# Up biases as the last row of the experts' weights, loads of 126 partitions, another order of products, and integer targets in the rows of a decoder layer's expert stage

## The chip, the cores and the metric

The kernel runs on one core of a Trainium2 chip. The metric is the device time of one execution in microseconds (us); less is better. The engines are named as in the profile: PE (TensorE) does matrix products, PEld is its loading of stationary operands, DVE is VectorE, ACT is ScalarE, POOL is GpSimd and SP is SyncE, which here only starts DMAs.

## The reference

One decoder layer with post-norms on x of shape (16, 128, 128): self-attention with 16 heads of 8, whose four projections are circulant matrices; a cross-attention ("xattn") over a context of 120 rows per batch; and a mixture of 8 experts, 2 per token, with a shared expert. Each is added to its input and followed by a layer norm without gain or offset:

```python
x = _layernorm(x + attn(x, ...))
x = _layernorm(x + xattn(x, ctx_1024, ...))
x = _layernorm(x + ffn(x, ...))

# ffn, on the 2048 rows xt of the normed x, D = 128, I = 256, E = 8
scores = softmax(xt @ gate_w.T)
idx = top_k(scores + gate_b, 2); weights = scores at idx
h = swiglu((xt @ w1[e] + b1[e]) * (xt @ w3[e] + b3[e]))      # 512 columns, h has 256
out = sum over the two e of weight * (h @ w2[e] + b2[e])  +  the same with the shared sw1, sb1, ... sb2
```

swiglu takes the even columns g and the odd columns l, clips both at 7, and gives g * sigmoid(1.702 g) * (l + 1). The rows that enter the ffn come straight from a layer norm, so the 128 elements of each sum to zero (to rounding).

## The kernel before, in words

**Front.** The 16 batches (128 tokens each) go through attention in 64 slots, four per batch (a slot is one group of 4 heads of one batch; the loops over `n` from FIRST_SLOT to LAST_SLOT, one per engine). In slot n PE computes scores (line 1321, 7 slots ahead), scores less their maximum (1331), and weighted values (1344, 1348); DVE takes row maxima (934), ACT the exponentials (766). Beside that the steps of the chain of earlier batches run: output projection, norm, cross-attention, norm (`chain`, `chain_steps`, steps 1 to 8). The two norms of a batch lie in the slots with n % 4 = 1 (step 1) and n % 4 = 3 (step 7): DVE computes the statistics (961, 963), POOL the root (`root`, 612 and 614), and DVE applies it in the next slot (995, 1004). Every engine goes through its instructions in the order of the code, so what is written ahead holds up what is behind.

**Loads.** SP issues all plain DMAs of this stage in the order of the slots (lines 480 to 528): the stacks of queries and keys, the rows of maxima (460), and between them the weights: `up_weights` (w1[e] and w3[e], 128 partitions x 512 each, into W1 and W3), in UP_SLOTS, `down_weights` in DOWN_SLOTS. The biases of all experts are loaded as 81 rows of 128, split by POOL into three bf16 parts (lines 682 to 688), written to DRAM and read back into three partitions for each of b1, b3, b2 (520 to 528). POOL halves the down weights (679, HALVE_SLOTS).

**Routing.** Four groups of four batches. `routing` on DVE picks the two experts of each token and the row of a buffer `xs` in DRAM for each of its two copies; POOL scatters the normed rows there by indirect DMA (`scatter`, line 634), each with two more columns written by `mark` (624, 625): the target row in `ys`, as a float, and the weight. Each expert's rows are padded to whole tiles of 128; the paddings hold a pad row whose target lies behind the real rows of ys.

**The shared expert** runs for the first 8 batches in the slots from 25 to 64 (`shared`, `shared_up`, `shared_products`, `shared_hidden`), transposed, with the up biases as per-partition columns, and for the last 8 as tiles.

**Tiles.** From slot 66 on, 47 tiles go through `tile` on PE, ACT and DVE: m = 0 to 7 are the shared expert on the last 8 batches, m = 8 to 46 are up to 39 tiles of routed rows, whose expert is read from a table (`bass.ds(e_up * I2, I2)`). In step m PE transposes the hidden rows of tile m - 2 (1492) and the input rows of tile m + 1 (1494), does the first up product of tile m (1501) with its bias (1502: a product of ones in three partitions and the three bf16 parts), the down product of tile m - 2 (1512) with its bias (1514), and the second up product of tile m with its bias. ACT copies the transposes (852), takes the tanh of tile m - 1 (855), copies the first up product (858) and scales the down product by the rows' weights (868). DVE multiplies, clips and gates (1071 to 1079). POOL scatters the result to ys (`place`, 712), and prepares the targets: `meta` copies the weight and turns the target into an integer, with a different place for paddings in each buffer (697 to 705). SP loads the rows (`load`, 478) into a ring of 4, behind `meta` of the row 4 back. The routing of the last group is put between the tiles m = 6 to 17 on DVE (LAST_ROUTING, LAST_TILES). Ahead of m = 7 the kernel waits for the scatter of the first three groups and the first loads.

**End.** SP waits for all of ys, loads it, PE sums, DVE and POOL do the last norm.

The change and the prediction's steps touch lines 463 to 478, 497 to 528, 584 to 605, 616 to 643, 679 to 713, 795 to 868, 1034 to 1080, and 1454 to 1528.

## Time and profile before

| | us |
|---|---|
| median of 3 runs | 418.36 (418.06 to 418.45) |
| the profiled execution | 419.23 |
| its span | 417.5 |
| PE busy | 347.8 (83%) |
| DVE busy | 282.4 (68%) |
| ACT busy | 175.2 (42%) |
| POOL busy | 195.5 (47%) |
| mean granted clock of TensorE | 0.956 |

The span is the time from the first to the last instruction; the execution's own time has some 1.7 us around it. The stages in this execution: up to about 30 us the first loads and projections, then the slots of attention up to about 257 us, the last of them beside the first tiles, the tiles up to about 392 us, the end up to 417.5. The busy time is an average over these stages, so the rows further on are cut by stretches. In a timeline row the first number is the start and the second the duration, both in us, and what stands in brackets is the engine's idle time before it and what ended that. In a row of one source line there are the least, the median and the greatest duration in ns, and the first and the last start.

### The profile page before, as it was taken

The numbers are of one execution on the slowest core, as the hardware profiler recorded it, in microseconds if no ns is written. First come the engines' busy times: TensorE is split into PE (matmuls) and PEld (weight loads), VectorE is DVE, ScalarE is ACT, GpSimd is POOL, SyncE is SP. The second block draws the span as 40 slices with busy tenths as digits, with TensorE's granted clock in tenths as the row PEclk, the third lists the DMA queues.
The fourth block names the chain that finished last, engine by engine and source line by source line (L and its number), as shares of the span: only waits on it lengthen the run. The fifth ranks groups of instructions, "written<-read, shape, count | busy, mean of one in ns | idle before, by whom it ended". The sixth has DMA issues, their size and how long they took to land.

```text
span 417.5 us, 8518 instructions
## 1 busy us (share of the span) xinstructions
PE 347.8 (83%) x2415; PEld 224.0 (54%) x2415; DVE 282.4 (68%) x834; ACT 175.2 (42%) x498; POOL 195.5 (47%) x377
## 2 busy tenths in 40 slices
PE   2637887887998987878978699899999999999790
...
GB/s 98 172 207 123 196 143 117 209 197 175 207 75 206 156 110 91 64 74 23 23 28 72 63 19 26 40 32 52 90 61 64 54 44 46 45 40 19 27 203 100
DMA packets 53197, 39.56 MB, mean 95 GB/s; under 512 B 7623, under 2 KB 46632, under 8 KB 53147
## 3 DMA queue, kind: packets, MB, share of 16 engines
...
## 4 chain that ended last, share of the span: by engine, by line
PE 50%; DVE 19%; issue 8%; DMA 7%; POOL 7%; SPq 6%; ACT 2%; ACTq 0%; POOLq 0%; DVEq 0%
PE pT L1501 9%; PE pS L1501 9%; PE pM L1512 5%; DVE negmax L934 3%; PE pO L1492 3%; PE pM L1307 2%; DVE inv_den L950 2%; PE pT L1502 2%; PE pS L1502 2%; PE pT L1478 2%; POOL rstd L614 2%; POOL xs L634 2%; PE pO L1344 2%; PE pT L1331 2%; PE pS L1321 2%
## 5 line engine op out<-in xcount | busy, mean ns | idle before, releaser
L712 POOL DMA_INDIRECT ys<-sim_rhs,row_dest x39 | 40.5, 1038 | 36.7 <-ACT sim_rhs L868 32.8
L766 ACT ACTIVATE PT<-pT 128x512 f32<-128x512 f32 x64 | 38.0, 593 | 36.5 <-PE pT L1331 36.1
L1501 PE MATMUL pT<-W,XH 128*128 (+1 forms) x94 | 50.5, 619 | 0.0
L934 DVE TENSOR_REDUCE negmax<-pS 128x4 f32<-128x512 f32 x64 | 43.4, 679 | 9.0 <-PE pS L1321 8.7
L1501 PE MATMUL pS<-W,XH 128*128 (+1 forms) x94 | 49.0, 604 | 0.0
L612 POOL TENSOR_SCALAR vareps<-meanvar 128x1 f32<-128x1 f32 x32 | 8.5, 264 | 86.6 <-DVE meanvar L963 86.3
L1321 PE MATMUL pS<-Kdiag,Qst 128*128 128x512 f32 x64 | 41.5, 655 | 4.9 <-DMA Kdiag<-parts_scr 4.1
L1071 DVE TENSOR_TENSOR PT<-pT,PT 128x512 f32<-128x512 f32 x47 | 32.4, 690 | 19.4 <-PE pT L1502 16.3
L852 ACT COPY XH<-pO 128x384 f32<-128x384 f32 x47 | 22.5, 479 | 46.6 <-PE pO L1494 39.9
L1512 PEld LDWEIGHTS pM<-W,XH 128*128 128x128 f32 x188 | 28.5, 194 | 18.1 <-issue 14.4
L634 POOL DMA_INDIRECT xs<-X,slot x32 | 33.5, 1048 | 7.5 <-issue 5.2
L1331 PE MATMUL pT<-Qdiag,Kst 128*128 128x512 f32 x64 | 30.8, 482 | 2.6 <-DMA Qdiag<-maxT 2.2
L1512 PE MATMUL pM<-W,XH 128*128 (+1 forms) x188 | 29.4, 279 | 1.3 <-ACT XH L852 1.3
L655 POOL TENSOR_TENSOR hq_x<-X1T,hqT 128x128 f32<-128x128 f32 x16 | 7.3, 456 | 49.0 <-ACT hqT L787 49.0
L1076 DVE SCALAR_TENSOR_TENSOR Vz<-Vz,XT 128x256 f32<-128x256 f32 x47 | 20.1, 427 | 14.1 <-ACT Vz L855 12.5
L858 ACT COPY PT<-pS 128x512 f32<-128x512 f32 x47 | 27.2, 580 | 2.4 <-PE pS L1502 2.2
L855 ACT ACTIVATE Vz<-XT 128x256 f32<-128x256 f32 x47 | 19.6, 417 | 19.4 <-DVE XT L1073 17.2
L1344 PE MATMUL pO<-PT,Vz 128*32 128x128 f32 x512 | 27.6, 289 | 0.0
L1348 PE MATMUL pO<-PT,head_ones 128*32 128x128 f32 x512 | 26.5, 280 | 0.0
L1492 PEld LDWEIGHTS pO<-ident,hid 128*128 128x128 f32 x94 | 12.2, 142 | 23.3 <-issue 16.7
L1492 PE MATMUL pO<-ident,hid 128*128 128x128 f32 x94 | 18.4, 277 | 4.5 <-issue 1.7
L1478 PE MATMUL pT<-W 128*128 128x512 f32 x32 | 21.0, 743 | 0.7 <-DVE XH L1043 0.7
...
## 6 DMA issues: line engine op xcount, KB each, us to landing
parts_scr<-qk_hi SPq DMA_DIRECT2D x16, 256.0 KB, 3.1
W<-in_L_ffn_w SPq DMA_DIRECT2D x16, 256.0 KB, 4.0
...
parts_scr<-qk_lo SPq DMA_DIRECT2D x8, 256.0 KB, 3.4
```

The source lines that it names most:

```text
L634: pool.indirect_dma_start(xs.ap(), bass.IndirectOffsetOnAxis(ap=slot[:, k, b:b + 1], axis=0), X2[:, b, :], None).then_inc(scat_sem(g), 16)
L712: pool.indirect_dma_start(ys.ap(), bass.IndirectOffsetOnAxis(ap=row_dest[:, k:k + 1], axis=0), YO[:, i % RING, :], None).then_inc(s_ysc[i ...
L766: act.activation(PT[:, u % 3, :], pT[:, 0, :], ACT.Exp, scale=SCALE).then_inc(p_sb, 1)
L934: dve.tensor_reduce(out=negmax[:, b % 2, HG * j:HG * (j + 1)], in_=pS[:, u % 2, :].rearrange("p (g k) -> p g k", g=HG), axis=AX.X, op=ALU.max,
L1071: dve.tensor_tensor(prod[:, p, :], pT[:, p, :], up1[:, p, :], ALU.mult).then_inc(prod_sb, 1)
L1321: pe.matmul(pS[:, u % 2, :], Qst[:, (b // 2) % 2, j, (b % 2) * P:(b % 2 + 1) * P], Kdiag[:, b % 2, j, :, :], start=True, stop=True).then_i ...
L1331: pe.matmul(pT[:, 0, :], Kst[:, (b // 2) % 2, j, (b % 2) * P:(b % 2 + 1) * P], Qdiag[:, b % 2, j, :, :], start=True, stop=True).then_inc(s ...
L1344: pe.matmul(pO[32 * hg:32 * hg + 32, 0:P], Vz[:, b % 2, hg, j, :], PT[:, u % 3, hg * P:(hg + 1) * P], start=(j == 0), stop=(j == U - 1), s ...
L1478: pe.matmul(pT[:, 1, :], (W1, W3)[step % 2][:, first:first + 2 * P - step // 2:2], x2_of[g], start=True, stop=True).then_inc(f_ps, 1)
L1492: mm = pe.transpose(pO[:, k * P:(k + 1) * P], hid[:, p, k * P:(k + 1) * P], ident[:])
L1501: pe.matmul(bank, XH[:, 1 - p, 2 * P:3 * P], W[:, bass.ds(e_up * I2, I2)], start=True, stop=False)
L1512: pe.matmul(pM[:, 0:D], XH[:, p, k * P:(k + 1) * P], W2[:, bass.ds(e_y * I + k * D, D)], start=(k == 0), stop=False)
```

## The change

The rows entering the experts sum to zero, so x[0] = -(x[1] + ... + x[127]), and x @ w = x[1:] @ (w[1:] - w[0]). The change uses this: the rows are taken as their elements 1 to 127 with a one behind them, the weights W1 and W3 as rows 1 to 127 less row 0, with the bias in the last row. So:

- `up_weights` loads rows 1 to 126 (126 partitions) and, in a second DMA, row 0 into all 128 partitions of a buffer; `up_biases` at slot 11 loads rows 127 and the biases of all experts into partitions 126 and 127. POOL subtracts in 18 slots (LESS_SLOTS: 16, 17, 24, 25, 29, 30, 34, 35, 39, 40, 44, 45, 49, 50, 54, 55, 59, 60), 127 x 512 each. The next load waits for the subtraction of the one before (one buffer).
- The weights' loads are at slots 13, 21, 26, ... 56 (before: 13, 15, 19, ... 35, and 67, 68).
- The matmuls of line 1502 are gone; the down bias is a product over 3 partitions instead of 128. In a tile the order is first up product, down bias, second up product, down product.
- The bias of b1 and b3 for the shared expert is in the weights too: ACT and DVE copy and multiply.
- The gate's weights are transformed likewise (two DVE operations at the slot -11).
- Rows in xs have 131 columns: target (int32) and weight in the last two. `meta` is gone; `place` takes the target from the loaded row, and paddings have the target 4096, which the scatter's bounds leave out. The ring of loaded rows has 8 places, and a load waits for the scatter of the row 8 back.

```diff
-BIAS_SLOTS = {7: 0, 11: 1, 15: 2}
-RING = 4
-XW = D + 2
+RING, XRING = 4, 8
+XW = D + 3
-UP_SLOTS = {**{15 + 4 * e: e for e in range(E - 2)}, 67: E - 2, 68: E - 1}
+UP_SLOTS = {13: E, **{21 + 5 * e: e for e in range(E)}}
+LESS_SLOTS = {n + 3 + k: (e, k) for n, e in UP_SLOTS.items() for k in range(2)}
+LESS_ORDER = {e: i for i, e in enumerate(UP_SLOTS.values())}
...
-            def up_weights(e, done):
-                a, c = (w1[e], w3[e]) if e < E else (sw1, sw3)
-                sp.dma_start(W1[:, e * I2:(e + 1) * I2], a).then_inc(done, 16)
-                sp.dma_start(W3[:, e * I2:(e + 1) * I2], c).then_inc(done, 16)
+            def up_weights(e):
+                i = LESS_ORDER[e]
+                if i:
+                    sp.wait_ge(w_less, 2 * i)
+                for k, (W, w) in enumerate(((W1, w1 if e < E else sw1), (W3, w3 if e < E else sw3))):
+                    first = e * D * I2 if e < E else 0
+                    sp.dma_start(W[0:P - 2, e * I2:(e + 1) * I2],
+                                 bass.AP(w.tensor, first + I2, [[I2, P - 2], [1, I2]])).then_inc(s_w_up, 16)
+                    sp.dma_start(first_rows_of[:, k, :], bass.AP(w.tensor, first, [[0, P], [1, I2]])).then_inc(s_w_up, 16)
+            def up_biases():
+                for W, routed, shared, b, sb_ in ((W1, w1, sw1, b1, sb1), (W3, w3, sw3, b3, sb3)):
+                    sp.dma_start(W[P - 2:P - 1, 0:E * I2].rearrange("p (e n) -> p e n", n=I2),
+                                 bass.AP(routed.tensor, (P - 1) * I2, [[0, 1], [D * I2, E], [1, I2]])).then_inc(s_w_bias, 16)
+                    sp.dma_start(W[P - 2:P - 1, E * I2:(E + 1) * I2], shared[P - 1:P, :]).then_inc(s_w_bias, 16)
+                    sp.dma_start(W[P - 1:P, 0:E * I2], b.rearrange("(o e) n -> o (e n)", o=1)).then_inc(s_w_bias, 16)
+                    sp.dma_start(W[P - 1:P, E * I2:(E + 1) * I2], sb_.rearrange("(o n) -> o n", o=1)).then_inc(s_w_bias, 16)
...
-                if r >= RING:
-                    sp.wait_ge(t_ps, NA + r - RING + 1)
-                    sp.wait_ge(meta_sb, r - RING + 1)
+                if r >= XRING:
+                    q = r - XRING
+                    sp.wait_ge(t_ps, NA + q + 1)
+                    sp.wait_ge(s_ysc[q % RING], 16 * (q // RING + 1))
...
+                if n in LESS_SLOTS:
+                    e, k = LESS_SLOTS[n]
+                    here = (W1, W3)[k][0:P - 1, e * I2:(e + 1) * I2]
+                    pool.wait_ge(s_w_up, 64 * (LESS_ORDER[e] + 1))
+                    pool.wait_ge(s_w_bias, 128)
+                    pool.tensor_tensor(here, here, first_rows_of[0:P - 1, k, :], ALU.subtract).then_inc(w_less, 1)
...
                 pool.wait_ge(y_sb, NA + 1 + i)
-                pool.wait_ge(meta_sb, i + 1)
-                pool.indirect_dma_start(ys.ap(), bass.IndirectOffsetOnAxis(ap=row_dest[:, k:k + 1], axis=0),
-                                        YO[:, i % RING, :], None).then_inc(s_ysc[i % RING], 16)
+                pool.indirect_dma_start(ys.ap(), bass.IndirectOffsetOnAxis(ap=XR[:, i % XRING, D + 1:D + 2].bitcast(I32), axis=0),
+                                        YO[:, i % RING, :], None, bounds_check=2 * TOKENS - 1,
+                                        oob_is_err=False).then_inc(s_ysc[i % RING], 16)
...
             for i in range(NR):
                 place(i)
-                if i + RING < NR:
-                    meta(i + RING)
...
-                    act.activation(lin_g, pT[:, 1, :], ACT.Identity, bias=b1_col[:, c, 0:1], scale=1.0).then_inc(f_out, 1)
+                    act.copy(lin_g, pT[:, 1, :]).then_inc(f_out, 1)
...
-                    dve.scalar_tensor_tensor(out=lin_g, in0=pT[:, 1, :], scalar=b3_col[:, c, 0:1], in1=lin_g, op0=ALU.add,
-                                             op1=ALU.mult).then_inc(f_out, 1)
+                    dve.tensor_tensor(lin_g, pT[:, 1, :], lin_g, ALU.mult).then_inc(f_out, 1)
...
-                def product(bank, W, k, done, free):
+                def product(bank, W, done, free):
 
                     if m >= 2:
                         pe.wait_ge(free, m - 1)
-                    pe.matmul(bank, XH[:, 1 - p, 2 * P:3 * P], W[:, bass.ds(e_up * I2, I2)], start=True, stop=False)
-                    pe.matmul(bank, bias_rows[:, k, :], bias3[:, bass.ds(e_up * I2, I2)], start=False,
+                    pe.matmul(bank, XH[:, 1 - p, 2 * P:3 * P], W[:, bass.ds(e_up * I2, I2)], start=True,
                               stop=True).then_inc(done, 1)
 
                 if up:
-                    product(pS[:, p, :], W1, 0, a_ps, up1_sb)
+                    product(pS[:, p, :], W1, a_ps, up1_sb)
+                if y:
+                    if m >= 3:
+                        pe.wait_ge(y_sb, m - 2)
+                    pe.matmul(pM[:, 0:D], three[:], b2_parts[:, bass.ds(e_y * D, D)], start=True, stop=False)
+                if up:
+                    product(pT[:, p, :], W3, b_ps, prod_sb)
                 if y:
                     pe.wait_ge(xh_sb, m + 2)
-                    if m >= 3:
-                        pe.wait_ge(y_sb, m - 2)
                     for k in range(2):
-                        pe.matmul(pM[:, 0:D], XH[:, p, k * P:(k + 1) * P], W2[:, bass.ds(e_y * I + k * D, D)],
-                                  start=(k == 0), stop=False)
-                    pe.matmul(pM[:, 0:D], bias_rows[:, 2, :], bias3[:, bass.ds(e_y * D, D)], start=False,
-                              stop=True).then_inc(y_ps, 1)
-                if up:
-                    product(pT[:, p, :], W3, 1, b_ps, prod_sb)
+                        mm = pe.matmul(pM[:, 0:D], XH[:, p, k * P:(k + 1) * P], W2[:, bass.ds(e_y * I + k * D, D)],
+                                       start=False, stop=(k == 1))
+                    mm.then_inc(y_ps, 1)
```

## Rows read from the trace of the kernel before

**Rows 1.** Busy time by stretches; each engine's busy us, TensorE's clock, DMA share, GB/s
```profile
77.00:100.00 23.00, 18.51 (x202) 13.58 (x201) 17.92 (x57) 9.94 (x36) 8.35 (x20) 1.00 0.74 210
263.30:300.30 37.00, 35.15 (x161) 19.48 (x160) 30.68 (x96) 17.75 (x44) 21.46 (x44) 1.00 0.20 54
300.30:385.20 84.90, 84.90 (x394) 49.82 (x393) 57.22 (x141) 47.58 (x112) 56.84 (x113) 1.00 0.17 47
```

**Rows 2.** Timeline, TensorE's matmuls of tile 19
```profile
303.00 0.38 PE L1492 MATMUL pO<-ident,hid 128*128 128x128 f32 x2
...
303.22 0.27 PE L1494 MATMUL pO<-ident,sim_add 128*128 128x128 f32 x1
...
303.33 1.02 PE L1501 MATMUL pS<-W,XH 128*128 x2
...
304.19 0.38 PE L1502 MATMUL pS<-bias,bias_rows 128*128 x1
...
304.41 0.61 PE L1512 MATMUL pM<-W,XH 128*128 x4
...
304.85 0.22 PE L1514 MATMUL pM<-bias,bias_rows 128*128 x1
...
304.91 1.08 PE L1501 MATMUL pT<-W,XH 128*128 x2
...
305.82 0.38 PE L1502 MATMUL pT<-bias,bias_rows 128*128 x1
...
306.04 0.38 PE L1492 MATMUL pO<-ident,hid 128*128 128x128 f32 x2
```

**Rows 3.** Timeline, the bias product of tile 46
```profile
386.00 0.38 PE L1502 MATMUL pS<-bias,bias_rows 128*128 x1
```

**Rows 4.** Timeline, VectorE's and ScalarE's work beside tile 19
```profile
302.07 0.37 ACT L868 ACTIVATE sim_rhs<-pM,row_weight 128x128 f32<-128x128 f32 x1
...
303.20 0.69 DVE L1071 TENSOR_TENSOR PT<-pT,PT 128x512 f32<-128x512 f32 x1 [0.97 <-issue]
...
303.53 0.48 ACT L852 COPY XH<-pO 128x384 f32<-128x384 f32 x1 [1.09 <-issue]
...
304.26 0.42 ACT L855 ACTIVATE Vz<-XT 128x256 f32<-128x256 f32 x1 [0.25 <-DVE XT L1073]
...
305.17 0.42 DVE L1079 SCALAR_TENSOR_TENSOR hid<-XT,Vz 128x256 f32<-128x256 f32 x1
```

**Rows 5.** GpSimd's addition by source line, and VectorE's operations beside it (source lines, timeline)
```profile
L642 POOL TENSOR_TENSOR X<-X x4: 1178/1193/1239, 178.3 to 272.4; 128x512 f32<-128x512 f32 x4
...
265.37 0.19 DVE L1110 TENSOR_TENSOR cand<-biased,rtop 128x32 f32<-128x32 f32 x1
...
272.72 0.96 DVE L1110 TENSOR_TENSOR cand<-biased,rtop 128x32 f32<-128x32 f32 x1
...
L1004 DVE TENSOR_SCALAR X<-R,meanvar,rstd x16: 345/473/2081, 67.2 to 254.1; 128x128 f32<-128x128 f32 x16
...
L1073 DVE TENSOR_SCALAR XT<-PT x47: 293/294/1268, 242.2 to 388.8; 128x256 f32<-128x256 f32 x47
```

**Rows 6.** Timeline, a halving of down weights and VectorE beside it
```profile
147.49 0.54 DVE L995 TENSOR_SCALAR X<-R,meanvar,rstd 128x128 f32<-128x128 f32 x1 [1.00 <-POOL rstd L614]
...
147.53 0.89 POOL L679 TENSOR_SCALAR W<-W 128x256 f32<-128x256 f32 x1
```

**Rows 7.** Waits from 77 to 235 us; total, times, longest
```profile
PE pX L1392 <- DVE X L995: 9.1, 9, 2.5
```

**Rows 8.** SP's load for the shared expert, slot 16's matmul (timeline), landing of weights (page)
```profile
73.75 0.43 SPq L465 DMA_DIRECT2D W<-in_L_ffn_sw  x1
...
77.63 0.40 PE L1331 MATMUL pT<-Qdiag,Kst 128*128 128x512 f32 x1
...
W<-in_L_ffn_w SPq DMA_DIRECT2D x16, 256.0 KB, 4.0
```

**Rows 9.** First up product of all tiles by source line; first and last start
```profile
L1501 PE MATMUL pS<-W,XH x94: 592/595/1061, 235.7 to 385.6; 128*128 x78, 128*128 128x512 f32 x16
```

159 lines of the change are left out of this document (58 added, 101 removed).

## The prediction

> **What bounds the kernel now.** I read the busy time of each engine by stretches first, then the groups of TensorE's instructions, the timeline of one tile, and the waits of the attention stage. The stretches [rows 1] show two regimes. From 300.30 to 385.20 us TensorE is busy for all of the 84.90 us while VectorE has 57.22: the expert stage is bound by TensorE. From 77 to 100 us no engine is full (TensorE 18.51, VectorE 17.92 of 23), the DMA engines are busy 0.74 of the time, and chains across engines set the pace. From 263.3 to 300.3 us both are loaded, because the routing of the last group runs on VectorE between the tiles.
>
> One tile on TensorE [rows 2], start to start: two transposes of the hidden rows 0.22, transpose of the inputs 0.11, first up product 0.86, **its bias 0.22**, down product 0.44, its bias 0.06, second up product 0.91, **its bias 0.22**: 3.04 us. The bias of tile 19 starts at 304.19 and that of tile 46 at 386.00 [rows 2, 3]: 27 periods in 81.81 us, 3.03 each.
>
> **Expert tiles.** The two up biases go into row 127 of the weights, so two matmuls of 512 columns leave each tile: 2 x 0.22 = 0.44. The down bias stays (a contraction over 3 partitions, which I cost as now: 128 columns stream through either way, bounds 0 and its 0.06). The period by TensorE is 3.03 - 0.44 = 2.59.
>
> Can the others follow? VectorE's chain of a tile starts at 303.20 and ends at 305.59 [rows 4]: 2.39 us, tanh on ScalarE inside it. It fits into 2.59 with 0.2 to spare. In the new order the second up product comes before the down product, so VectorE gets its input about 0.44 earlier in the period; but ScalarE's scaling of the down result (0.37) now comes at the end, ahead of the next copy of the transposes. Laid end to end from the start T of a tile: the down product starts at T + 2.16 (the sum of what comes before it) and takes 0.61, so it is done at T + 2.8; scaling to 3.2, copy (0.48) to 3.73, tanh (0.42) to 4.15, two VectorE products (0.43 each, with their gaps) to 5.1; the transposes that need it start at T + 2 x 2.59 = 5.18. It fits by 0.1, so TensorE stays the bound. GpSimd loses its two or three small operations per tile, which nothing waits for. **27 x 0.44 = -11.9 us.** Bounds: -11.9 and, if ScalarE's position costs 0.15 a tile, -7.8.
>
> Tiles 7 to 18: the first up product of tile 7 starts at 263.3, where that stretch of [rows 1] begins, and that of tile 19 at 303.33 [rows 2]: 12 periods take 40.0 us where 12 x 3.03 = 36.4 would do; what is over is VectorE's routing. VectorE's chain of 2.39 times 12 is 28.7, and its 30.68 busy us in the 37 [rows 1] with gaps and the waits for tanh leave it close to full. Between 0 and 12 x 0.44 = 5.3 us can be gained; I take -1.5, near the VectorE end. The tiles of the shared expert end in a wait for the scatter of group 2, GpSimd's indirect writes and two transfers; only about two are ahead of that on the path: -1.0 (0 to -2.6). At the end the last second up product comes about 0.6 us sooner: -0.6 (0 to -1.2). In the attention stage the bias scalings of ScalarE and VectorE become plain copies and products, and a dozen small DMAs and five small GpSimd operations go: -0.3 (0 to -1). The paddings left out of the scatter are writes nobody waits for; only the last tiles' scatter is on the path, and its 2 us are latency: 0. The gate's extra subtraction (two VectorE operations before slot -11) lies beside the load of the context: 0, at most +0.5 if that is landed already. Gains together: **-15.3 us**.
>
> **The subtractions.** What is new is a GpSimd TENSOR_TENSOR of 127 x 512 in 18 slots between 16 and 60 (the first weight row off all others, once for each of 9 experts and 2 matrices). The nearest row is the addition of 128 x 512 on GpSimd: 4 of them, 1.19 us each [rows 5]. GpSimd has that time (8.35 busy of 23 in the first row of [rows 1]). What matters is what VectorE does meanwhile. VectorE's TENSOR_TENSOR of line 1110 takes 0.19 at 265.37 and 0.96 at 272.72, beside the addition that starts at 272.4; its TENSOR_SCALAR of line 1004 takes 0.345 at least and 2.08 at most, that of line 1073 0.29 and 1.27 [rows 5], and these longest ones lie beside additions too. So VectorE stands still for some 1.0 us per addition wherever it has an operation from SBUF to SBUF next. Against that, the halving of the down weights, a GpSimd TENSOR_SCALAR of 0.89, has the TENSOR_SCALAR beside it take only 0.54 instead of 0.35 [rows 6].
>
> The Trainium skill, SBUF — State Buffer, section "Who interferes with whom", says that GpSimd and VectorE share one pair of ports as an exclusive lock: an operation of VectorE in a two-port mode or with two SBUF inputs and one of GpSimd exclude each other for the whole instruction. By it each subtraction locks out up to its 1.19 us, 21 us in all, and so would the halvings, whose row shows 0.2; the rows of the additions agree with it.
>
> A subtraction is of the additions' kind, so I take 1.0 at the ten in slots with routing (25, 29, 30, 39, 44, 45, 54, 55, 59, 60), where such operations come every few tenths, and 0.75 at the other eight: 16 us of VectorE standing still. How much reaches the end? In slots 17, 25, 29 and 49 the subtraction is queued straight behind the root of the first norm, for whose result VectorE's line 995 waits, and TensorE waits for that: 9 waits, 9.1 us [rows 7]. There nearly all of it arrives. In slots 35, 55 and 59 it falls on line 1004 in the same way, with lines 1001 and TensorE's transpose behind it. In the others VectorE's idle fifth and the 7 slots by which the scores run ahead take part of it. I take a bit over half: **+8.5 us**; bounds 0.1 x 18 = +1.8 (the halvings' price) and 18 x 1.19 = +21.4.
>
> **The loads.** Each pair of 256 KB becomes two of 252 KB and two of 256 KB (the first row in all partitions): +4.6 MB, between slots 13 and 56, and GpSimd now waits for them in the slot 3 later, with its roots behind that wait. SP issues without a pause there: line 465 of slot 13 goes out at 73.75, and the matmul of slot 16 starts at 77.63 [rows 8]. Ahead of the last of those loads come 6 more DMAs at slot 11 (8 for 2) and 2 more of its own, 0.43 us each: 3.4 us later, about 78.5, and with 4.0 us to landing [rows 8] about 82.5. GpSimd wants to go on at 78, and TensorE needs the root of slot 17 at about 82. At slots 21/24 the same but smaller; later SP is in step and the DMA engines have room. SP also stands in the wait for the previous subtractions, with the prefetches of attention behind it, which have 3 to 4 slots' time. **+2.0 us**, bounds -1 (the loads at 15, 19 and 23 are gone) and +6.
>
> **Sum.** -15.3 + 8.5 + 2.0 = -4.8. The profiled execution took 419.23 (span 417.5 and 1.7 around it), so 414.4 of its kind; the median of the runs is 418.36, 0.9 lower: **413.6 us**. About 0.2%, 0.84 us, is what a measurement of this kernel can tell from no change.
>
> **Rivals.**
> 1. *The lock reaches the end in full (slower).* Place: the 18 slots of the subtractions. For it: the four additions, and the in-order waits of [rows 7]. Against it: VectorE is idle a fifth of that stage. From 0.75 us per subtraction on the path (13.5 us, with +2.0 for the loads) the gain of 15.3 is used up. At 1.0 each and +3 for the loads: -15.3 + 18 + 3 = +5.7, **424 us**. By the skill's rule taken strictly it is this case. Chance 0.2.
> 2. *The subtractions are hidden*, as the halvings are: -15.3 + 1.8 + 0.5 = -13, **405.4 us**. For it [rows 6]; against it [rows 5]. Chance 0.2.
> 3. *ScalarE's and VectorE's loop binds the tiles*, at some 2.75 instead of 2.59: 4.1 us less gained, **417.7 us**. Against it the 0.1 us of room above; for it, that this room is small and GpSimd's scatter falls on VectorE's clipping. Chance 0.12.
> 4. *The change doesn't do what it says:* the scatter that checks its bounds takes GpSimd over 2.6 us where it takes about 1 now, and GpSimd sets the period of the tiles; at 3.03 nothing is gained there: +7, **425.5 us**. No row shows such a scatter. Chance 0.03.
>
> My case has 0.45. It and the second hold 0.65, nearly all faster. Faster 0.68, same 0.07 (the third and the edge of mine), slower 0.25. Cases of both signs don't hold it evenly; the range from the second to most of the first is 404.5 to 422. My case alone: 409 to 417.5.
>
> **What the profile after would show.** The two starts of the up products 0.22 and the period near 2.59, TensorE still busy without a gap, confirm the tiles; a wait for VectorE's hidden rows ahead of the transposes is rival 3. Operations of VectorE of 1.2 to 1.5 us beside the 18 subtractions confirm the lock, and the start of the first up product of the shared tiles (235.7 now, [rows 9]) says what arrived: about 246 by my case, 237 by rival 2, over 254 by rival 1. A wait of GpSimd for a load at slots 16 and 24 confirms the loads. I am wrong if the tiles' period is off by over 0.1, or if that start moves by less than 5 or more than 15 us.

## The result and the profile after

| | before | after |
|---|---|---|
| median of the runs (4 of each) | 418.21 (417.68 to 418.45) | 435.73 (434.90 to 437.58) |
| span of the profiled execution | 417.5 | 435.8 |
| mean granted clock of TensorE | 0.956 | 0.92 |

The changed kernel is slower: ratio 1.0439, interval 1.0401 to 1.0477. The prediction was 413.6, range 404.5 to 422.

The profiled execution of the changed kernel took 437.58, 1.9 us over its median, so the span is 18.3 us longer where the medians differ by 17.5. Where the 18.3 us came from is read by laying the starts of the same work beside each other. A slot is dated by its matmul of the scores less their maximum (line 1331 before, 1311 after), a tile by its first up product; all starts are in us.

| | slot 16 | 17 | 25 | 36 | 48 | 63 | tile 0 | tile 20 | tile 46 | end |
|---|---|---|---|---|---|---|---|---|---|---|
| before | 77.6 | 81.0 | 103.7 | 140.2 | 177.0 | 222.0 | 235.7 | 306.4 | 385.1 | 417.5 |
| after | 79.1 | 88.6 | 115.0 | 151.7 | 195.1 | 247.1 | 261.7 | 330.5 | 404.4 | 435.8 |
| late by | 1.4 | 7.6 | 11.3 | 11.5 | 18.1 | 25.1 | 26.0 | 24.2 | 19.3 | 18.3 |

26.0 us are lost before the first tile; 1.8 come back in tiles 0 to 20, 4.9 in tiles 20 to 46, 1.0 at the end. The first tile's start is also one row of a view, the source line of the up products of the kernel after (least, median and greatest ns, first and last start); it answers to [rows 9], 235.7:

```profile
L1482 PE MATMUL pS<-W,first_rows_of x94: 592/595/1061, 261.7 to 404.8; 128*128 x78, 128*128 128x512 f32 x16
```

**The tiles.** The timeline of the kernel after, TensorE's matmuls of one tile, which answers to [rows 2]:

```profile
358.66 0.38 PE L1473 MATMUL pO<-ident,hid 128*128 128x128 f32 x2
358.88 0.27 PE L1475 MATMUL pO<-ident,sim_add 128*128 128x128 f32 x1
358.99 1.02 PE L1482 MATMUL pS<-W,first_rows_of 128*128 x2
359.94 0.22 PE L1491 MATMUL pM<-b_parts,three 3*128 x1
360.10 1.12 PE L1482 MATMUL pT<-W,first_rows_of 128*128 x2
361.06 0.61 PE L1497 MATMUL pM<-W,first_rows_of 128*128 x4
361.51 0.27 PE L1473 MATMUL pO<-ident,hid 128*128 128x128 f32 x1
```

Start to start: 0.22, 0.11, 0.95, 0.16, 0.96, 0.45, together 2.85. The two up biases are gone, as predicted, but the first up product takes 0.95 where it took 0.86, the down bias 0.16 where it took 0.06, the second up product 0.96 where it took 0.91: 0.24 us given back around one product of 3 partitions. Its weight loads show why (timeline of the kernel after, the loading of stationary operands in the same tile; in brackets the idle time before):

```profile
358.88 0.30 PEld L1482 LDWEIGHTS pS<-W,first_rows_of 128*128 128x128 f32 x2
359.94 0.09 PEld L1491 LDWEIGHTS pM<-b_parts,three 3*128 3x128 bf16 x1 [0.76 <-issue]
360.10 0.30 PEld L1482 LDWEIGHTS pT<-W,first_rows_of 128*128 128x128 f32 x2
```

The load of the 3-partition operand stands at 359.94, where its matmul does, after 0.76 us in which the loader idled beside a running product; the next load stands at 360.10, where its own matmul does. Neither is hidden behind a matmul. Over the stage TensorE is busy without a gap (windows of the kernel after, columns as in [rows 1], the last row there; this one is tile 19 to 46, 26 periods of 2.84 within it from tile 20 on):

```profile
326.60:404.40 77.80, 77.80 (x332) 42.38 (x331) 56.03 (x137) 46.07 (x109) 29.76 (x30) 1.00 0.17 47
```

**The attention stage, first loss.** Rows of the timelines of GpSimd, TensorE and SP of the kernel after, about slots 16 and 17:

```profile
78.67 0.45 SPq L469 DMA_DIRECT2D W<-in_L_ffn_sw  x1
80.04 0.37 SPq L471 DMA_DIRECT2D first_rows_of<-in_L_ffn_sw  x1
80.51 1.83 SPq L439 DMA_DIRECT2D Kdiag<-parts_scr  x4
...
87.01 1.26 POOL L675 TENSOR_TENSOR W<-W,first_rows_of 127x512 f32<-127x512 f32 x1 [6.47 <-DMA first_rows_of<-in_L_ffn_sw]
...
87.89 0.76 PE L1301 MATMUL pS<-Kdiag,Qst 128*128 128x512 f32 x1 [6.33 <-issue]
```

GpSimd waited 6.5 us for the load, as one check of the prediction had it, but TensorE stood 6.3 us as well, and not for GpSimd's root: the matmul that ends its wait is a scores product, which reads the diagonal stack of the keys (`Kdiag`). That stack is issued by SP at 80.51, right behind the four DMAs of up weights and first rows (1 MB). The windows of the same stretch (first TensorE busy, and after POOL the granted clock, DMA share, GB/s):

```profile
82.00:88.00 6.00, 0.11 (x1) 0.14 (x1) 1.40 (x5) 0.75 (x4) 0.99 (x1) 0.57 1.02 268
88.00:96.00 8.00, 8.00 (x51) 6.08 (x52) 3.60 (x7) 2.26 (x8) 3.21 (x6) 0.50 0.52 148
```

The DMA engines are full while every other engine is nearly idle. Then the clock stands at half, 1.2 GHz, for 8 us in which TensorE is busy for all of them; in the kernel before it was 1.00 over these 8 us. The kernel is 7.6 us late at slot 17 and 10.2 late at slot 19.

**Second loss, VectorE.** Timeline of the kernel after, a subtraction with the operation of VectorE beside it, twice:

```profile
92.37 1.27 POOL L675 TENSOR_TENSOR W<-W,first_rows_of 127x512 f32<-127x512 f32 x1
92.44 1.28 DVE L977 TENSOR_SCALAR X<-R,meanvar,rstd 128x128 f32<-128x128 f32 x1 [1.00 <-POOL rstd L610]
...
149.46 1.27 POOL L675 TENSOR_TENSOR W<-W,first_rows_of 127x512 f32<-127x512 f32 x1 [1.68 <-DMA first_rows_of<-in_L_ffn_w]
149.48 0.75 DVE L900 SCALAR_TENSOR_TENSOR qk_lo<-pM,qk_bias,qk_hi 128x512 fp32r<-128x512 f32 x1 [1.37 <-ACT qk_hi L741]
```

The norm at 92.44 takes 1.28 instead of some 0.35 and ends within 0.1 us of the subtraction. At 149.48 VectorE reads one of its operands from PSUM and takes its usual 0.75 beside a subtraction. Of the 18 subtractions 14 have an operation of VectorE beside them that is 0.7 to 1.8 us over its usual length; those excesses add up to some 14.7 us. Twice, with 1.8 each, the operation began before the subtraction did, beside a scatter of GpSimd, and ended with the subtraction (timeline):

```profile
188.28 1.10 POOL L630 DMA_INDIRECT xs<-X,slot  x1 [0.29 <-POOL X L621]
188.68 2.17 DVE L965 SCALAR_TENSOR_TENSOR wx<-wqv,hc 128x128 f32<-128x128 f32 x1
189.41 1.27 POOL L675 TENSOR_TENSOR W<-W,first_rows_of 127x512 f32<-127x512 f32 x1
```

The groups by line from 77 to 260 us (busy us, mean ns, idle before):

```profile
L675 POOL TENSOR_TENSOR W<-W,first_rows_of 127x512 f32<-127x512 f32 x18 | 22.9, 1275 | 10.2 <-DMA first_rows_of<-in_L_ffn_sw 6.5 <-DMA first_rows_of<-in_L_ffn_w 3.7
...
L965 DVE SCALAR_TENSOR_TENSOR wx<-wqv,hc 128x128 f32<-128x128 f32 x13 | 9.5, 732 | 0.0
```

And TensorE's waits of the kernel after from 77 to 262 us (total, times, longest), beside [rows 7]:

```profile
PE pX L1372 <- DVE X L977: 11.4, 9, 1.9
PE pS L1301 <- issue: 9.6, 2, 6.3
PE pX L1380 <- DVE A L983: 5.5, 8, 2.3
PE pX L1393 <- DVE wx L965: 4.7, 5, 2.1
```

The 9.6 in two waits are the loads (slots 17 and 25); nearly all of the rest shown is VectorE. From here two theories had to be told apart for the 26 us, and one more for the tiles.

### The profile page after: what moved, and what is told of

Its sections match the earlier page's. It is cut to its first block, busy times and chain, and to the rows that moved or that the text cites. A ratio compares the mean times of both kernels' runs of the same rounds, so it can differ in the third digit from the quotient of the medians.

```text
span 435.8 us, 8151 instructions
## 1 busy us (share of the span) xinstructions
PE 348.6 (80%) x2321; PEld 221.4 (51%) x2321; DVE 297.1 (68%) x836; ACT 176.0 (40%) x498; POOL 181.5 (42%) x286
## 4 chain that ended last, share of the span: by engine, by line
PE 48%; DVE 24%; issue 10%; POOL 6%; DMA 5%; SPq 3%; ACT 2%; POOLq 0%; ACTq 0%; DVEq 0%
PE pT L1482 10%; PE pS L1482 8%; PE pM L1497 5%; DVE negmax L916 4%; PE pM L1287 3%; PE pO L1473 3%; DVE inv_den L932 2%; POOL rstd L610 2%; PE pT L1311 2%; PE pO L1324 2%; DVE stats L943 2%; PE pM L1491 2%; DMA X<-in_x 2%; DVE X L986 1%; DVE wx L965 1%
## 5 line engine op out<-in xcount | busy, mean ns | idle before, releaser
L697 POOL DMA_INDIRECT ys<-sim_rhs,sim_add x39 | 39.1, 1003 | 63.8 <-ACT sim_rhs L848 61.4
L1482 PE MATMUL pT<-W,first_rows_of 128*128 (+1 forms) x94 | 52.9, 644 | 0.0
L1482 PE MATMUL pS<-W,first_rows_of 128*128 (+1 forms) x94 | 49.0, 603 | 0.0
L608 POOL TENSOR_SCALAR vareps<-meanvar 128x1 f32<-128x1 f32 x32 | 8.6, 269 | 85.1 <-DVE meanvar L945 85.0
L1497 PEld LDWEIGHTS pM<-W,first_rows_of 128*128 128x128 f32 x188 | 28.3, 192 | 22.7 <-issue 22.0
L1311 PE MATMUL pT<-Qdiag,Kst 128*128 128x512 f32 x64 | 32.6, 510 | 1.4 <-DMA Qdiag<-maxT 1.0
L1497 PE MATMUL pM<-W,first_rows_of 128*128 (+1 forms) x188 | 29.1, 278 | 0.6 <-ACT first_rows_of L834 0.5
L848 ACT ACTIVATE sim_rhs<-pM,sim_add 128x128 f32<-128x128 f32 x39 | 14.3, 367 | 35.0 <-PE pM L1497 34.9
L675 POOL TENSOR_TENSOR W<-W,first_rows_of 127x512 f32<-127x512 f32 x18 | 22.9, 1275 | 10.2 <-DMA first_rows_of<-in_L_ffn_sw 6.5
L834 ACT COPY first_rows_of<-pO 128x384 f32<-128x384 f32 x47 | 22.5, 478 | 7.8 <-PE pO L1475 7.0
L1301 PEld LDWEIGHTS pS<-Kdiag,Qst 128*128 128x128 f32 x64 | 14.3, 225 | 21.5 <-issue 21.2
L837 ACT ACTIVATE Vz<-XT 128x256 f32<-128x256 f32 x47 | 19.7, 418 | 11.2 <-DVE XT L1051 11.1
```

Of the source, the lines that this page charges most:

```text
L697: pool.indirect_dma_start(ys.ap(), bass.IndirectOffsetOnAxis(ap=XR[:, i % XRING, D + 1:D + 2].bitcast(I32), axis=0), YO[:, i % RING, :], N ...
L1301: pe.matmul(pS[:, u % 2, :], Qst[:, (b // 2) % 2, j, (b % 2) * P:(b % 2 + 1) * P], Kdiag[:, b % 2, j, :, :], start=True, stop=True).then_i ...
L1311: pe.matmul(pT[:, 0, :], Kst[:, (b // 2) % 2, j, (b % 2) * P:(b % 2 + 1) * P], Qdiag[:, b % 2, j, :, :], start=True, stop=True).then_inc(s ...
L1482: pe.matmul(bank, XH[:, 1 - p, 2 * P:3 * P], W[:, bass.ds(e_up * I2, I2)], start=True, stop=True).then_inc(done, 1)
L1497: mm = pe.matmul(pM[:, 0:D], XH[:, p, k * P:(k + 1) * P], W2[:, bass.ds(e_y * I + k * D, D)], start=False, stop=(k == 1))
```

## The experiments

The kernels were run in four groups, each group on one chip (another for each) beside the kernel before, whose median in them was 417.39 (e1 to e4), 418.55 (b1, f4, f1, f2), 417.62 (b2, b3, f3, g1) and 417.83 (h1 to h3). Between groups the ratios compare better than the medians. Where an experiment leaves work out, its expectation says what.

### One part of the change at a time, taken away

**e1_k128.** The down bias over 128 partitions, zeros behind the third; the rest of the changed kernel stays.

```diff
-        three = sb("three", [3, P], BF16)
-        b2_parts = sb("b2_parts", [3, (E + 1) * D], BF16)
+        three = sb("three", [P, P], BF16)
+        b2_parts = sb("b2_parts", [P, (E + 1) * D], BF16)
```

> The changed kernel, with the down bias as a product over 128 partitions (ones in three partitions of the stationary operand, the others and the other rows of the biases zero) instead of over 3. Theory A: the product over 3 partitions keeps TensorE from loading weights under the running matmul, which costs 0.25 us a tile (2.85 instead of the 2.59 that the removal of two bias products gives); then the period is 2.59 to 2.62 and the time 435.7 - 47 x 0.25 = about 424. Rival: the period is set by the loop of ScalarE and VectorE or by the new order of products; then it stays at 2.85 and the time at 435 to 436.

Measured: 432.91, ratio 1.0358 (1.0294 to 1.0422). From tile 20 to 46 the period is 67.9 / 26 = 2.61. But 2.0 us of the gain were lost again between tiles 18 and 20: timelines of e1_k128, SP and TensorE:

```profile
314.20 11.54 SPq L541 DMA_DIRECT2D xs<-pad_row  x8
327.21 1.18 SPq L494 DMA_DIRECT2D sim_add<-xs  x2
...
328.79 0.44 PE L1477 MATMUL pO<-ident,hid 128*128 128x128 f32 x2 [2.65 <-DMA sim_add<-xs]
```

The eight pad rows go out in one block behind load 11, which in the changed kernel waits for the scatter of the row 8 back (in the kernel before they went out from 289.99 to 299.81, in time). The next loaded rows come late. The term for the product of 3 partitions is confirmed by the period; the time missed the expected 424, and a fourth cost turned up.

**e2_onecol.** The subtractions cut to one column of 512, with all waits kept.

```diff
-                    pool.tensor_tensor(here, here, first_rows_of[0:P - 1, k, :], ALU.subtract).then_inc(w_less, 1)
+                    pool.tensor_tensor(here[:, 0:1], here[:, 0:1], first_rows_of[0:P - 1, k, 0:1], ALU.subtract).then_inc(w_less, 1)
```

> The changed kernel, with each of the 18 subtractions on GpSimd narrowed from 512 columns to 1 (so the weights are not made less their first row; loads, waits and order stay). Theory B: the subtractions hold VectorE up by the shared ports, 0.5 to 1 us each on the path after slot 19; then the first up product of the tiles (261.7 in the changed kernel, 235.7 before) comes at 249 to 253, and the time is 423 to 427. Rival: the loads and the waits for them make the whole loss; then the time is 433 or more.

Measured: 429.65, ratio 1.0247 (1.0206 to 1.0289). The first tile starts at 248.6, 13.0 us behind before and 13.1 ahead of the kernel after; behind slot 25 the delay hardly grows (9.2 there, 11.9 at slot 63, where the kernel after goes from 11.3 to 25.1). So the subtraction is worth 13 us of the 26, and most of what is left arises by slot 25. The time missed the expected 423 to 427: it gave back only 6.1 by the medians (8.0 by the ratios), because tiles 18 to 20 lost 5.1 us to a wait for loaded rows, as in e1_k128.

**e3_norows.** The first rows are not loaded; a buffer of zeros is subtracted instead.

```diff
-                    sp.dma_start(first_rows_of[:, k, :], bass.AP(w.tensor, first, [[0, P], [1, I2]])).then_inc(s_w_up, 16)
```

> The changed kernel without the DMAs that load the first row of each matrix into all partitions (4.7 MB less; the subtractions stay and take zeros instead, so the results differ). Theory C: the doubled volume of the loads holds up the keys' transfer at slot 17 and the subtraction at slots 16 and 24, 7 us at slot 17 and 2 to 3 at slot 25; then the delay at slot 19 (10.2 us in the changed kernel) falls to 2 to 4 and the time is 425 to 428. Rival: only the wait of GpSimd for the loads of 126 partitions or the 16 single-partition DMAs matters, then the delay at slot 19 stays over 7.

Measured: 439.32, ratio 1.0508 (1.0478 to 1.0539), a miss: 425 to 428 was expected, and a delay of 2 to 4 at slot 19, where it is 6.5. Slot 25 is 5.9 late instead of 11.3, slot 36 7.1 instead of 11.5, but by the first tile it is 23.0, and tiles 18 to 20 lose 3.8. With half of the bytes of these loads gone, which is all that the change had added to them, TensorE's wait at slot 17 is 2.6 instead of 6.3; of the 5.4 us won by slot 25 the first tile keeps 3.0. The wait that is left has the bytes of the kernel before ahead of it, but SP issues them at 77.7 here, where the shared expert's load went out at 73.75 before [rows 8].

**e4_shift.** Loads and subtractions one slot later, by which the loads stand behind the diagonal of the keys in SP's queue.

```diff
-UP_SLOTS = {13: E, **{21 + 5 * e: e for e in range(E)}}
+UP_SLOTS = {14: E, **{22 + 5 * e: e for e in range(E)}}
```

> The changed kernel with all up loads (and with them the subtractions) one slot later, at slots 14, 22, 27, ... 57, so that at slots 14 and 22 SP issues the transfer of keys (Kdiag) before them and not behind them. If the stall of 6.3 us at slot 17 is the keys' transfer queued behind 1 MB of weights, the delay at slot 19 falls from 10.2 to 3 to 6 us and the time to 429 to 432. If it is GpSimd's wait for the load ahead of the root of slot 17 (or the DMA engines' volume as such), it only moves by a slot and the time stays at 434 to 437.

Measured: 436.94, ratio 1.0465 (1.0416 to 1.0515). Slot 17 is 2.2 late (after: 7.6), slot 25 1.2 (11.3), slot 36 0.8 (11.5): the same bytes at the same pace, behind the keys instead of ahead of them, cost nothing up to there. It is the place in the queue that cost 10 us up to slot 25, not the volume by itself. Yet between slots 36 and 48 the delay goes from 0.8 to 12.5, where subtractions, halvings and scatters stand close together on GpSimd; that they are the cause was not tried by itself. The first tile still comes 6.4 us sooner than in the kernel after; then tiles 18 to 20 take 4.4 us longer than before, where the kernel after lost nothing, and the median shows no gain at all (429 to 432 was expected).

### What the tiles are worth

**b1_nobias.** The kernel before without its two up-bias products in the tiles.

```diff
-                    pe.matmul(bank, XH[:, 1 - p, 2 * P:3 * P], W[:, bass.ds(e_up * I2, I2)], start=True, stop=False)
-                    pe.matmul(bank, bias_rows[:, k, :], bias3[:, bass.ds(e_up * I2, I2)], start=False,
-                              stop=True).then_inc(done, 1)
+                    pe.matmul(bank, XH[:, 1 - p, 2 * P:3 * P], W[:, bass.ds(e_up * I2, I2)], start=True,
+                              stop=True).then_inc(done, 1)
```

> The kernel before without the two bias products of 512 columns in the tiles' up products (the up biases of the routed experts and of the shared tiles are left out of the result). It prices what the change takes out of a tile, with nothing else touched. My sum gave 0.44 a tile: the period goes 3.03 to 2.59 and the time to 418.2 less some 13 to 14 us, 404.5. If VectorE or ScalarE sets the period before that (the third rival, 2.75), it is 408.5. If the 0.44 of a bias product was only there because nothing else ran on TensorE, nothing is gained: 418.

Measured: 408.06, ratio 0.9767 (0.9680 to 0.9855). The period from tile 20 to 46 is 71.0 / 26 = 2.73, not 2.59. The time is the one that I had worked out for the third rival, but not by its mechanism: from 301 to 372 us TensorE has one wait, of 0.9 us, for a loaded row, and none for ScalarE or VectorE. The products themselves stand further apart in this order.

**b3_order.** The same, with the down product behind the second up product.

```diff
                 if up:
                     product(pS[:, p, :], W1, 0, a_ps, up1_sb)
+                if up:
+                    product(pT[:, p, :], W3, 1, b_ps, prod_sb)
                 if y:
...
-                if up:
-                    product(pT[:, p, :], W3, 1, b_ps, prod_sb)
```

> As the run b1_nobias (no up biases in the tiles, 408.06, period 2.71 to 2.73), with the down product moved behind the second up product, as in the change. If the order is what brings the changed kernel with 128 partitions to 2.60, the period is 2.60 here too and the time 404 to 406; if it is the free ring or the missing target work of GpSimd, it stays at 2.7 and 408.

Measured: 405.74, ratio 0.9710 (0.9651 to 0.9770), period 67.9 / 26 = 2.61. The medians' intervals overlap, so the time does not separate the two; the periods do. The period of 2.59 that I worked out needs the new order as well as the missing biases.

**b2_k3.** The kernel before, with the down bias as a product over 3 partitions and nothing else changed.

```diff
-                    pe.matmul(pM[:, 0:D], bias_rows[:, 2, :], bias3[:, bass.ds(e_y * D, D)], start=False,
+                    pe.matmul(pM[:, 0:D], bias_rows[0:3, 0, :], bias3[0:3, bass.ds(e_y * D, D)], start=False,
```

> The kernel before, with only the down bias of the tiles turned into a product over 3 partitions (it reads the parts of b1, so the down bias of the result is another). Theory: a stationary operand of 3 partitions is not loaded while the product before it runs, nor is the next one while it runs, and that costs 0.2 to 0.25 us in every tile; the period then goes from 3.03 to 3.2 to 3.3 and the time from 418.5 to 425 to 430. Rival: the 0.25 seen in the changed kernel is from its order of products (the down bias ahead of the second up product); then nothing changes here, 418.5.

Measured: 425.52, ratio 1.0191 (1.0145 to 1.0238); period 85.1 / 26 = 3.27 where it was 3.03. One product of 128 columns with a contraction over 3 instead of 128 partitions makes the kernel before 2% slower. Timeline of b2_k3, TensorE's matmuls and its loads:

```profile
344.49 0.22 PE L1514 MATMUL pM<-bias,bias_rows 3*128 x1
344.65 1.13 PE L1501 MATMUL pT<-W,XH 128*128 x2
...
344.49 0.09 PEld L1514 LDWEIGHTS pM<-bias,bias_rows 3*128 3x128 bf16 x1
344.64 0.30 PEld L1501 LDWEIGHTS pT<-W,XH 128*128 128x128 f32 x2
```

Again each load stands at its own matmul's start. With 128 partitions (f4_c, below; same view) the bias is loaded 0.43 us ahead of its matmul, the second up product's weights beside the bias's matmul, and 0.06 us are enough from one start to the next:

```profile
328.78 0.22 PE L1495 MATMUL pM<-b_parts,three 128*128 x1
328.84 1.08 PE L1486 MATMUL pT<-W,first_rows_of 128*128 x2
...
328.35 0.10 PEld L1495 LDWEIGHTS pM<-b_parts,three 128*128 128x128 bf16 x1 [0.24 <-issue]
328.78 0.30 PEld L1486 LDWEIGHTS pT<-W,first_rows_of 128*128 128x128 f32 x2 [0.33 <-issue]
```

The Trainium skill, TensorE: Matmul & The Clock Gate, section "LDWEIGHTS (loading the stationary operand)", says that the contraction's length does not matter for the load's duration. The rows agree: 0.09 us for 3 partitions, 0.10 for 128. What differs is whether the load is pulled ahead.

### The two causes of the attention stage as a square

These four kernels all have the down bias over 128 partitions and the eight pad rows spread two by two over loads 11 to 14:

```diff
-                if r == PAD_LOAD:
+                if PAD_LOAD <= r < PAD_LOAD + 4:
                     sp.wait_ge(pad_sb, 1)
-                    for e in range(E):
+                    for e in (2 * (r - PAD_LOAD), 2 * (r - PAD_LOAD) + 1):
```

They differ in the order of the loads (slots as in the change, or the edit of e4_shift) and in the subtraction (whole, or the edit of e2_onecol).

**f4_c**, loads behind the keys, subtractions whole:

> The changed kernel with three of its costs taken away together: the down bias contracted over 128 partitions (zeros behind the third), the loads of the up weights one slot later (so that they stand behind the diagonal of the keys in the queue of SP), and the eight pad rows written two each between loads 11 to 14 rather than all behind load 11. The subtractions stay whole on GpSimd. If the three were separate and additive: 435.7 less 5 (27 x 0.22 less what the pads took back), less about 6 for the loads, and no wait of TensorE at tiles 18 to 20: 423 to 426. If the lock alone decides the attention stage, the first up product stays 20 us or more behind that of before and the time is over 428.

**f1_free**, loads behind the keys, one column:

> As the run f4_c, but each subtraction is narrowed to one column of 512 (so the up products of the experts are not those of the reference); the waits and the order stay. Theory: the lock of GpSimd's 1.27 us block on VectorE is what is left of the delay in the attention stage. Then the first up product of the tiles comes within 5 us of that of before (235.7) and the time is 408 to 413, some 12 to 14 below f4_c. Rival: the delay is from the DMAs (4.6 MB more and their waits); then it stays at +10 or more and the time within 4 us of f4_c.

**h1_order**, loads ahead of the keys, whole:

> The changed kernel with the down bias over 128 partitions and the pad rows spread over four loads; the up weights' loads stay in their slots, ahead of the keys' diagonal in SP's queue, and the subtractions whole on GpSimd. Against f4_c (421.5), which differs only in the slots of the loads. If the order of the loads costs by itself, the first tile starts 5 to 8 us later than in f4_c (254.1) and the time is 427 to 430. If the subtractions only take other slots to cost the same (as e4_shift would have it), it starts within 2 us of f4_c and the time is 421 to 424.

**h3_col**, loads ahead of the keys, one column:

> As the run h1_order, each subtraction narrowed to one column (the experts' up products are not those of the reference). Against f1_free (407.8, first tile at 238.5) it prices the order of the loads without the block: if the stalls of 6.3 and 3.3 us at slots 17 and 25 go through, the first tile starts at 246 to 249 and the time is 415 to 419. Additive causes would give h1_order less 13.7; if the two share their slack, it is more.

| median us, ratio (interval); first tile's start | subtraction whole | one column | difference |
|---|---|---|---|
| loads ahead of the keys | h1_order 434.24, 1.038 (1.0309 to 1.0451); 260.0 | h3_col 419.42, 1.0028 (0.9995 to 1.0061); 249.4 | 14.8; 10.6 |
| loads behind the keys | f4_c 421.49, 1.0045 (1.0005 to 1.0085); 254.1 | f1_free 407.81, 0.973 (0.9666 to 0.9794); 238.5 | 13.7; 15.6 |
| difference | 12.7; 5.9 | 11.6; 10.9 | |

The first tile's start is one row of the source line of the up products, for f4_c, f1_free, h1_order and h3_col:

```profile
L1486 PE MATMUL pS<-W,first_rows_of x94: 592/595/1061, 254.1 to 390.7; 128*128 x78, 128*128 128x512 f32 x16
```

```profile
L1486 PE MATMUL pS<-W,first_rows_of x94: 592/595/1062, 238.5 to 375.3; 128*128 x78, 128*128 128x512 f32 x16
```

```profile
L1486 PE MATMUL pS<-W,first_rows_of x94: 592/595/1062, 260.0 to 402.1; 128*128 x78, 128*128 128x512 f32 x16
```

```profile
L1486 PE MATMUL pS<-W,first_rows_of x94: 592/595/1062, 249.4 to 389.7; 128*128 x78, 128*128 128x512 f32 x16
```

The profiled execution of h3_col took 422.2, 2.8 over its median, so what is read from its trace alone is uncertain by that much. By the medians the two causes add up: the subtraction costs about 14 us, the order of the loads about 12, whichever way the other stands (by the ratios, since the two rows are of different groups: 13.2 to 14.7, and 12.5 to 14.0). h1_order came out above the 427 to 430 expected, though its first tile lies where it was expected. By the first tile's start the order is worth less (5.9 and 10.9), and the difference lies in tiles 20 to 30. In the profiled executions of h1_order and h3_col a scaling of ScalarE waits there 4.4 us for the scatter that reads the buffer it writes, once each; TensorE waits behind it, and in h1_order the clock falls (mean 0.86 from 328 to 340). f4_c and f1_free do not show it. Timeline of h1_order, ScalarE:

```profile
332.65 0.37 ACT L852 ACTIVATE sim_rhs<-pM,sim_add 128x128 f32<-128x128 f32 x1 [4.45 <-remote]
```

It stands where the spread pad rows are written (SP issues the last two at 331.2). The same wait is in the profile of h2_hybrid, which has its loads behind the keys, so it is not the order's alone; what makes that scatter late was not tried. Whether all of the 12 us is owed to the stall at slots 17 and 25, or some of it to this wait coming more often, stays open; 6 to 11 us is what the first tile shows.

### Doing the subtraction otherwise

**f2_dve**, as f4_c, but `dve.tensor_tensor` at the end of the same slots, none on GpSimd.

> As the run f4_c, but the subtractions are done whole on VectorE at the end of the same slots, GpSimd doing none. VectorE then gives some 0.6 to 0.7 us for each of 18 rather than stand still for up to 1.27: if the lock is the cost, the first up product comes 3 to 8 us sooner than in f4_c and the time is 415 to 421, between f1_free and f4_c. If the cost is GpSimd's own time (the roots of the norms queued behind 1.27 us) the gain is larger still, to 413. If neither, the time is that of f4_c or above, as VectorE is the fuller engine.

Measured: 417.09, ratio 0.9933 (0.9891 to 0.9975), first tile at 248.4: 5.7 us ahead of f4_c, 9.9 behind f1_free. By the medians it is 4.4 us faster than f4_c. VectorE does each in 0.69 us, half of GpSimd's time (groups by line of f2_dve, 60 to 260 us), and `wx` beside it is back from 732 ns to 368:

```profile
L1232 DVE TENSOR_TENSOR W<-W,first_rows_of 127x512 f32<-127x512 f32 x18 | 12.3, 685 | 4.3 <-DMA first_rows_of<-in_L_ffn_w 3.4 <-DMA first_rows_of<-in_L_ffn_sw 0.8
...
L962 DVE SCALAR_TENSOR_TENSOR wx<-wqv,hc 128x128 f32<-128x128 f32 x16 | 5.9, 368 | 1.3 <-ACT hc L769 1.3
```

The idle time in the first row belongs to the price: VectorE, which goes in the order of the code, waited 4.3 us for the loads that it subtracts. In one piece of 3.4 us before 111.33 TensorE stood 2.9 us behind it.

**f3_pieces**, as f4_c, each subtraction in four of 128 columns on GpSimd.

```diff
+                    for q in range(4):
+                        part = slice(q * I2 // 4, (q + 1) * I2 // 4)
+                        pool.tensor_tensor(here[:, part], here[:, part], first_rows_of[0:P - 1, k, part], ALU.subtract).then_inc(w_less, 1)
```

> As the run f4_c (421.5), each subtraction on GpSimd cut into four of 128 columns. If VectorE is shut out for a whole instruction and can slip in between two, it waits 0.3 us at a time rather than 1.27, and with four fixed costs GpSimd is busy somewhat longer (some 1.6 us for four): 413 to 419. If GpSimd holds on to the port while its next instruction is queued, the four count as one longer block: 422 to 426.

Measured: 416.09, ratio 0.9959 (0.9928 to 0.9990), first tile at 243.5. GpSimd is busy longer with it, 30.8 us instead of 22.9, and the kernel is 5.4 us faster than with whole blocks by the medians, 3.6 by the ratios. (Its profiled execution, 412.92, is 3.2 us under its median, so its first tile is an early one.) Timeline and groups by line of f3_pieces:

```profile
85.16 1.74 POOL L681 TENSOR_TENSOR W<-W,first_rows_of 127x128 f32<-127x128 f32 x4
85.23 0.47 DVE L983 TENSOR_SCALAR X<-R,meanvar,rstd 128x128 f32<-128x128 f32 x1 [1.00 <-POOL rstd L614]
...
L681 POOL TENSOR_TENSOR W<-W,first_rows_of 127x128 f32<-127x128 f32 x72 | 30.8, 458 | 2.1 <-DMA first_rows_of<-in_L_ffn_w 2.0
```

The same norm that took 1.28 beside a whole block takes 0.47 beside four pieces that last 1.74 together. Here VectorE waits for one instruction of GpSimd, not for its busy time. It does not always get in between: in two of the 18 slots an operation of usually 0.2 took 1.66 (at 178.11, begun 0.3 ahead of the pieces) and 1.64, as long as all four (timeline of f3_pieces):

```profile
221.65 1.68 POOL L681 TENSOR_TENSOR W<-W,first_rows_of 127x128 f32<-127x128 f32 x4
221.75 1.64 DVE L1100 TENSOR_TENSOR pick<-iota,rtop 128x32 f32<-128x32 f32 x1
```

**g1_slots**, as f2_dve, both subtractions of an expert in one slot in which VectorE had over 1 us idle.

```diff
+UP_SLOTS = dict(zip((14, 19, 23, 31, 35, 39, 46, 51, 59), (E, *range(E))))
+LESS_SLOTS = dict(zip((18, 22, 30, 34, 38, 45, 50, 58, 62), (E, *range(E))))
```

> As the run f2_dve (417.1: loads behind the keys' diagonal, down bias over 128 partitions, pad rows spread, subtractions on VectorE), with both subtractions of an expert in one slot, and in slots where VectorE had over 1 us idle (18, 22, 30, 34, 38, 45, 50, 58, 62), loads right after the subtraction before. If VectorE's idle time in these slots can be used, half of the 10 us that f2_dve pays over f1_free comes back: 411 to 414. If what a subtraction delays is the chain behind it, wherever it stands, it is 416 to 418.

Measured: 416.88, ratio 0.9959 (0.9920 to 0.9998), first tile within 0.1 us of that of f2_dve. By the expectation that speaks for the chain and against the idle time. But the edit moved the loads too, and the profile shows a loss ahead of slot 25 that f2_dve does not have: slot 24 is 8.8 late where f2_dve has 2.1, and TensorE waits there for the rows of maxima, which SP issued behind four DMAs of weights (timelines of g1_slots, SP and TensorE):

```profile
98.41 0.37 SPq L469 DMA_DIRECT2D W<-in_L_ffn_w  x1
101.89 1.17 SPq L458 DMA_DIRECT2D Qdiag<-maxT  x2
...
109.03 0.47 PE L1316 MATMUL pT<-Qdiag,Kst 128*128 128x512 f32 x1 [2.75 <-DMA Qdiag<-maxT]
```

From slot 25 to the first tile g1_slots loses 4.1 us where f2_dve loses 11.2, some 3 of them by its wait before 111.33. So whether VectorE's idle time in a slot can be used stays open; a run with the loads where f2_dve has them would tell.

**h2_hybrid**, pieces on GpSimd up to slot 41, whole subtractions on VectorE from slot 45.

```diff
+                if n in LESS_SLOTS and n < 43:
...
+                if n in LESS_SLOTS and n >= 43:
...
+                    dve.tensor_tensor(here, here, first_rows_of[0:P - 1, k, :], ALU.subtract).then_inc(w_less, 4)
```

> The run f4_c with the subtractions of slots 17 to 41 on GpSimd in four pieces each, and those of slots 45 to 61 whole on VectorE. In f3_pieces the slots up to 43 cost nothing (its slot 43 at 161.1, before at 161.7) and those behind it 8 us; in f2_dve it is the other way round, 9.5 up to slot 43 and 3 behind it. If the costs belong to the slots, this kernel's first tile starts at 236 to 240 and the time is 407 to 411, as with one column; if the runs merely differ in luck, it lies with f3_pieces and f2_dve at 414 to 417.

Measured: 418.41, ratio 1.0011 (0.9980 to 1.0042), first tile at 244.2. A miss: the best halves of two profiles don't add up. Its slot 43 is 2.5 late where f3_pieces had it 0.6 early, with the same code up to there, so differences of some 3 us between single profiled executions carry no cause, and the best of several single profiles is an early one in part by luck.

## Why the prediction was wrong

The prediction's view of what bounds each stretch held; its sum had three wrong terms and one missing. Against the span, in us:

| term | predicted | measured |
|---|---|---|
| first tile's start (subtractions 8.5, loads 2.0, small gains -0.3) | +10.2 | +26.0 |
| tiles 0 to 18 or 20 | -2.5 | -1.8 |
| the tiles behind | -11.9 | -4.9 |
| end | -0.6 | -1.0 |
| sum | -4.8 | +18.3 |

1. **The down bias over 3 partitions, costed "as now" (0 to 0.06).** This step failed, and with an argument that sounds sound: 128 columns stream through either way. They do; what is lost is the loading of weights beside a running product, ahead of it and behind it. It costs 0.23 to 0.24 us in every tile, shown three ways: 2.84 to 2.61 without it in the changed kernel, 3.03 to 3.27 with it alone in the kernel before, and in the rows of the loads. With it 27 x 0.44 was never to be had; what came was 26 x 0.188 = 4.9.
2. **"A bit over half" of the subtractions' 16 us reaches the end.** VectorE's standing still was sized well (some 14.7 us of excess counted in the trace, 16 predicted). The share was not: 13.7 to 14.8 us by the medians, 10.6 to 15.6 by the first tile, so nearly all. I had taken VectorE's idle fifth and the lead of the scores as cover, and no run shows that they cover anything. The first rival had this mechanism, with a chance of 0.2: it named 0.75 us per subtraction on the path as the point where the gain is used up and took 1.0, and the medians give 0.76 to 0.82 each. My list of the subtractions right behind a root left out the one of slot 39. The Trainium skill, SBUF — State Buffer, section "Who interferes with whom", adds to its lock that whoever issues first gets the port. I had set [rows 6], where a halving cost VectorE 0.2, against it. In that row VectorE's operation starts 0.04 us ahead of GpSimd's, so it may have held the port itself; the row was no evidence that GpSimd's blocks are cheap. Nor was the longest one of line 1004 [rows 5], 2.08, the price of an addition alone: it began at 237.69 beside a scatter of GpSimd from 237.35, and the addition followed at 238.48. The same section says that an operation with at most one input in SBUF passes, outside the two-port modes; the row at 149.48 agrees, a length of 0.75 beside a full block.
3. **The loads, +2.0 with bounds -1 to +6.** I followed who waits for the load itself (GpSimd, then the root of slot 17) and left out who stands behind it in SP's queue. That was the diagonal of the keys for the scores 7 slots ahead. It cost 6.2 us at slot 17 and 2.7 at slot 25, with a stretch at half the clock behind the first; by the square it is worth 5.9 and 10.9 by the first tile and 11.6 and 12.7 by the medians, at my upper bound of 6 or over it. Not every execution stalls alike: TensorE's wait at slot 17 is 6.3 us in the kernel after and h3_col, 4.3 in e2_onecol and h1_order. e4_shift shows that one slot's shift takes it away.
4. **The missing term: loads behind the pad rows.** The new wait of SP (load r for the scatter of row r - 8) is named in the change and had no place in my sum. It cost nothing in the profile of the changed kernel, but 2.0 to 5.1 us between tiles 18 and 20 in e1_k128, e2_onecol, e3_norows and e4_shift, each of which had won time elsewhere. The wait and the place of the eight pad rows in one block were not taken away one by one; with the pad rows spread and the wait kept, f4_c and f1_free lose nothing there. That is why e4_shift, whose first tile was 6.4 us sooner, had nothing to show in its median, and why the causes had to be taken away together.
5. **What held, and the signs.** Both signs of being wrong that the prediction named came: the period of the tiles was off by 0.25 and the first tile moved by 26.0. The two up biases leave a tile as 0.44; once the 3 partitions are gone, the period is 2.60 (f4_c: 67.6 / 26; f1_free the same), against 2.59 worked out, and ScalarE's and VectorE's loop does not bind it in the new order; so the third rival is out. (My sum for that loop has a slip: 3.2 and a copy of 0.48 make 3.68, not 3.73, so the room was 0.15, not 0.1.) The fourth is too: a bounds-checked scatter takes 1.00 us on average. The second rival, subtractions hidden, is what f1_free emulates: 407.8 against 405.4.

So the idea of the change is worth 10.7 us (f1_free) if the subtraction cost nothing, and the kernel as written paid some 14 for it, some 12 for the place of nine loads in a queue, and 6.5 (27 x 0.24) for three partitions. These prices are not additive to the end: together they make +21.8 where the medians differ by 17.5. h1_order, which takes the three partitions away and spreads the pad rows, is only 1.5 us under the changed kernel (2.5 by the ratios), since its tiles 20 to 46 take 72.5 us where those of f4_c take 67.6, with the wait of 4.4 us among them; what causes that wait stays open. Versions that compute everything end at 0.9933 (f2_dve), 0.9959 (f3_pieces and g1_slots), 1.0011 (h2_hybrid) and 1.0045 (f4_c) of the kernel before. The best are 0.4 to 0.7% faster than it, with intervals that end just under 1; that is far less than the 2.7% of f1_free.
